# Scores copied out of PSUM by VectorE instead of ScalarE in an attention kernel with a computed position bias

## What is computed

```python
pos  = grid_q[:, :, None, :] - grid_kv[:, None, :, :]          # 1024 queries x 64 keys, x and y
bias = jnp.sign(pos) * jnp.log1p(jnp.abs(pos))
bias = relu(bias @ cpb_w1 + cpb_b1)                            # first layer, 2 -> 32
bias = relu(bias @ cpb_w2 + cpb_b2)                            # second layer, 32 -> 32
bias = (bias @ cpb_w3 + cpb_b3).reshape(b, 8, 1024, 64)        # third layer, 32 -> 1
sim  = einsum('bhid,bhjd->bhij', qh, kh) + bias
out  = einsum('bhij,bhjd->bhid', softmax(sim), vh)             # then projection, residual, MLP, residual
```

## Time and profile before

| | us |
|---|---|
| runs of the kernel before | 897.69, 897.99, 899.03 (median 897.99) |
| the profiled execution | 897.46, of which span from first to last instruction 895.7 |
| busy: PE, DVE, ACT, POOL | 814.1, 712.5, 675.4, 66.1 |
| mean granted TensorE clock | 0.975 of full speed |

### The profile page before, as it was taken

How to read it: one execution, slowest core, us unless ns; L and a number is a source line. 1 busy time by engine, 2 the same in 40 slices (tenths; PEclk the granted TensorE clock), 3 DMA queues, 4 the chain that set the end, 5 groups by cost and what they waited for, 6 DMA issues and landing times.

```text
span 895.7 us, 27530 instructions
## 1 busy us (share of the span) xinstructions
PE 814.1 (91%) x12470; PEld 232.7 (26%) x12470; DVE 712.5 (80%) x498; ACT 675.4 (75%) x775; POOL 66.1 (7%) x39
## 2 busy tenths in 40 slices
PE   2399998899999999789999999889999999999997
PEld 1122222232222222223222222222222222222224
DVE  4888798797877588888885868879888668989843
ACT  2468788878776688897876877797878678888863
POOL 3300031300000004030000000311000000000000
PEclk7599999999999999999999999999999999999999
DMA  4502020020110202002020200202002020200000
GB/s 163 120 2 49 2 48 4 12 65 3 43 34 1 48 3 49 12 3 65 2 63 15 49 1 3 49 12 53 15 4 61 14 48 2 72 3 2 2 15 25
DMA packets 18264, 27.67 MB, mean 31 GB/s; under 512 B 10980, under 2 KB 11620, under 8 KB 18148
## 3 DMA queue, kind: packets, MB, share of 16 engines
q1 hardware_dynamic: 18148, 25.91, 11.8%
HBM read 23.05 MB, written 2.74 MB: 29 GB/s over the span
## 4 chain that ended last, share of the span: by engine, by line
issue 59%; PE 26%; POOL 6%; ACT 5%; DVE 3%; DMA 0%; SPq 0%; ACTq 0%; POOLq 0%
PE pair L892 9%; PE scores L910 8%; POOL conv_prod L357 4%; ACT h L489 3%; POOL big L470 2%; PE pair L866 2%; DVE h L643 2%; PE pair L1045 1%; PE scores L921 1%; PE pair L1000 1%; PE pair L1018 1%; PE pair L1036 1%; PE scores L1006 1%; ACT big L591 0%; DMA const<-consts_dram 0%
## 5 line engine op out<-in xcount | busy, mean ns | idle before, releaser
L643 DVE TENSOR_TENSOR h<-hxy 128x2048 f32<-128x2048 f32 x256 | 578.4, 2288 | 76.5 <-PE pair L892 72.4
L489 ACT ACTIVATE h<-pair 128x1024 f32<-128x1024 f32 x512 | 517.2, 1023 | 143.5 <-PE pair L866 108.1
L892 PE MATMUL pair<-h,wts 32*32 32x512 f32 x8192 | 300.1, 603 | 17.0 <-ACT h L489 5.5
L910 PE MATMUL scores<-h,wts 128*32 128x512 f32 x2048 | 277.5, 610 | 0.1
L866 PE MATMUL pair<-fy,u_rows 32*128 32x512 bf16 x1024 | 103.1, 389 | 14.5 <-DMA fy<-fy_dram 14.5
L866 PEld LDWEIGHTS pair<-fy,u_rows 32*128 32x128 bf16 x1024 | 26.4, 91 | 233.6 <-issue 233.6
L892 PEld LDWEIGHTS pair<-h,wts 32*32 32x32 f32 x8192 | 66.1, 103 | 78.9 <-ACT h L489 34.5
L910 PEld LDWEIGHTS scores<-h,wts 128*32 128x32 f32 x2048 | 42.4, 108 | 157.5 <-issue 148.8
L357 POOL TENSOR_TENSOR conv_prod<-qpad,wts 128x288 f32<-128x288 f32 x16 | 34.0, 2150 | 426.5 <-ACT qpad L516 426.5
L1000 PE MATMUL pair<-const,probs 128*128 128x128 f32 x128 | 21.2, 291 | 21.5 <-ACT h L489 20.8
L499 ACT ACTIVATE probs<-scores,wts 128x512 f32<-128x512 f32 x32 | 22.0, 688 | 23.8 <-PE scores L910 23.5
(11 more groups left out here) (101 smaller groups left out, 376.0 us busy)
## 6 DMA issues: line engine op xcount, KB each, us to landing
hxy<-features_dram SPq DMA_DIRECT2D x64, 256.0 KB, 4.9
wts<-weights_dram SPq DMA_DIRECT2D x2, 960.0 KB, 8.1
att_den<-reciprocals_dram SPq DMA_DIRECT2D x7, 256.0 KB
x<-x_dram SPq DMA_DIRECT2D x2, 512.0 KB, 5.5
fy<-fy_dram SPq DMA_DIRECT2D x16, 64.0 KB
fy_dram<-fy_part SPq DMA_DIRECT2D x24, 32.0 KB, 3.8
out_dram<-x SPq DMA_DIRECT2D x3, 256.0 KB, 5.4
features_dram<-pos_sign SPq DMA_DIRECT2D x4, 128.0 KB, 2.3
```

The lines of the kernel that those rows point to most:

```text
L489: emptied("z", 2 * g + j, act.activation(h2[j][g % H2_BUFS][:].rearrange("p r n -> p (r n)"), pair_of("z", 2 * g + j)[:], ACT.Relu))
L643: dve.tensor_tensor(h1[g % H1_BUFS][:].rearrange("p c (y x) -> p c y x", x=W), hx[unit % 2][:, :, t].unsqueeze(2).broadcast_to([128, CT, H ...
L892: ins = pe.matmul(z_of(g, r)[32 * c:32 * (c + 1)], w(l, "w2")[key_rows(r), key_rows(r)], h1[g % H1_BUFS][key_rows(r), c], start=r >= 2, st ...
L910: ins = pe.matmul(scores[phase % 2][32 * r:32 * (r + 1)], w(l, "w3")[:, 32 * t:32 * (t + 1)], h2[rows[0] // 2][step % H2_BUFS][:, r % 2], ...
```

## The change

`copy_scores` moves from ACT to DVE and becomes a tensor-scalar add with the same operands. It gets a slot: 3, that is behind `first_layer(G+1)` and ahead of `first_layer(G+2)`, one slot ahead of `score_max`. Its three waits (the scores full, the products of queries and keys added, the earlier readers of `probs` done) move with it and now stand in DVE's list. Where a slot holds several stages, they follow in the order in which `plan` enters them: the stages behind a segment (`residual2`, `divide`) first, then those of the softmax, `hidden_terms`, and those of the next segment (`hats`).

```diff
-SOFTMAX_SLOTS = {("pe", "scores_t"): 2, ("dve", "score_max"): 4, ("act", "widen_max"): 3,
+SOFTMAX_SLOTS = {("dve", "copy_scores"): 3, ("pe", "scores_t"): 2, ("dve", "score_max"): 4, ("act", "widen_max"): 3,
                  ("pe", "max_off"): 4, ("act", "exp"): 4}
...
-            def copy_scores(phase):
-                unit, h = phase // 2, phase % 2
-                seg = unit // PAIRS
-                act.wait_ge(bias_added, STRIDES * (phase + 1) + 1)
-                act.wait_ge(qk_added, phase + 1)
-                if seg:
-                    wait_filled(act, "attend", 2 * (seg - 1) + h)
-                act.activation(probs[:, unit % PAIRS, bank(h)], scores[phase % 2][:], ACT.Identity, bias=w(seg // B, "b3"))\
-                    .then_inc(scores_copied, 1)
...
-                if g > STRIDES and g % STRIDES == 1 and g <= ALL_STEPS + 1:
-                    copy_scores(g // STRIDES - 1)
...
+            def copy_scores(phase):
+                unit, h = phase // 2, phase % 2
+                seg = unit // PAIRS
+                dve.wait_ge(bias_added, STRIDES * (phase + 1) + 1)
+                dve.wait_ge(qk_added, phase + 1)
+                if seg:
+                    wait_filled(dve, "attend", 2 * (seg - 1) + h)
+                dve.tensor_scalar(probs[:, unit % PAIRS, bank(h)], scores[phase % 2][:], w(seg // B, "b3"), None, ALU.add)\
+                    .then_inc(scores_copied, 1)
...
-                      "score_max": score_max, "divide": divide, "reciprocal": reciprocal,
+                      "copy_scores": copy_scores, "score_max": score_max, "divide": divide, "reciprocal": reciprocal,
```

## The result

The changed kernel takes 912.85 us (median of 4 runs, 911.56 to 914.74) against 898.51 for the kernel before on the same chip: a ratio of 1.0161, 95% interval 1.014 to 1.0182. That is slower, as forecast, but by 14 us and not by 5, and outside the range of 899.0 to 908.0. The profiled execution took 912.67, span 910.9, mean granted clock 0.972.

What follows compares the result with a forecast made beforehand. PE, busy 91% of the span, sets the time. Terms 0.36 - 3.42 - 2.01 - 0.42 + 0.15 - 0.06 gave 5.4 us lost: 903.4 beside the median of 897.99 (902.9 profiled); 8-in-10 range 899.0 to 908.0.

Steps and rivals of the forecast that it cites:

- the copy: Tensor-scalar out of PSUM on DVE: 0.75 us long, 0.67 from its start to the next DVE instruction (its turn).
- plain phases: 18 ordinary phases: layer3(G-1) to layer2(G+1) takes 3.66 us instead of 3.68, a gain of 0.02 each, 0.4 in all.
- divide in the chain: 6 phases (7 and 0) where divide stands ahead of score_max: loss 0.57 us each, 3.4 in all.
- the backlog: Phase 2 of segment 0, where DVE runs seven tiles without a pause: loss 0.42 us.
- the tail: The last phase, with nothing beside it: the copy takes 0.75 us for 0.69, loss 0.06.
- ACT's gain is taken by DVE's chain: Plain phases: ACT's relief lets PE run 0.29 us earlier, but copy, tile and maximum in sequence on DVE take it.
- layer2's wait for the maximum: Sign of being right: about 0.3 us in plain phases, 0.8 in six with divide, over 1 behind the convolution.
- Phase 4, 3 phases: Copy ahead of hats in slot 43; score_max at 389.70 against 389.75: gain 0.05 us each, 0.15 in all.
- Behind the convolution: Phase 3 of segments 0 to 2: DVE is late, so the copy's whole 0.67 us adds to layer2's wait; 2.0 in all.
- the clock: Rival, 20%: granted clock falls behind the convolution after longer PE idle time, costing 1 to 5.2 us; 904.4 to 908.6.
- the faster copy: Rival, 12%: out of PSUM the copy takes 0.42 to 0.55 us, say 0.48; 3.2 us gained, 894.8.
- PE did keep its clock in phase 4: Rival, 15%: earlier transposes keep PE's lead and clock in three phases 4, 2 us gained each; 897.4 to 903.

Runs made afterwards that it cites:

- E3: The changed kernel with score_max ahead of divide in the slots that hold both; 910.17 us, ratio 1.0128.
- E11: The changed kernel with phase 2 of segments 0 to 2 copied by ACT, phase 3 still by DVE; 910.37 us, ratio 1.0133.
- E6: The changed kernel with copy and score_max both last in slot 3, ahead of first_layer(G+2); 918.46 us, ratio 1.0221.
- E10: The kernel before, with copy and score_max early on DVE (slot 3) in 16 plain phases only; 894.96 us, ratio 0.9965.
- E1: The changed kernel with the copy behind hats, not ahead, in phase 4 of segments 0 to 2; 906.85 us, ratio 1.009.
- E9: The kernel before, ACT still copying, with only the copy's wait added in its slot on DVE, no work behind it; 902.88 us, ratio 1.0045.
- E2: The changed kernel with phase 3 of segments 0 to 2 copied by ACT; 909.21 us, ratio 1.0115.
- E8: The changed kernel with phase 3's copy in segments 0 to 2 one slot earlier, behind conv_sum and ahead of the tile; 913.04 us, ratio 1.0162.

## Why the prediction was wrong

Right, with sizes: the copy (0.75 taken, 0.750 measured; turn 0.67 and 0.67); plain phases (gain 0.02 forecast, 0.03 measured, as layer2's starts have it); divide in the chain (0.57; 0.58, and E3 shows that it is divide's place); the backlog (0.42; 0.40, gone in E11); the tail (0.06; 0.07). Also the reading that ACT's gain is taken by DVE's chain: E6 and E10 get the 0.29 us that were said to be there as soon as the tile leaves the chain. Of the signs that it named, layer2's wait for the maximum is 0.19 in plain phases for 0.3, 0.8 in those with divide as given, and behind the convolution, for "over 1 us", nothing, since layer3 at half clock covers it (0.82 in E3, where the clock holds). One sign of being wrong came true: PE waits for tiles of `first_layer`.

Wrong, the step "Phase 4, 3 phases ... Gain 0.05". It followed DVE's list to score_max, found that the copy fits into the idle time (it does, 4.54 for 4.50), and took the list behind score_max as unchanged. The idle time was not empty: POOL's products ran in it. With hats, which release them, 1.8 us later against layer3 and no idle time left ahead of score_max, POOL runs into the tile and the second hats, and these get 1.1 us longer each. That makes -1.5 a phase for +0.05, 4.85 us in all. Shown by E1 (hats back ahead: loss gone, same work) and E9 (hats held by a wait alone: 0.8 to 1.1 of loss, with POOL's 9.9 us in two of three segments). Two sentences of the forecast came near: that DVE's tiles leave 0.08 us at step 48, and that POOL shares DVE's list in time; they were used only to doubt a gain.

Too small, the term "Behind the convolution", 0.67 a phase. It is the right price of that phase's own copy (E11: 0.65, 0.66). It lacks the 0.3 to 0.5 by which phase 2's copy delays the convolution through POOL, DVE and POOL in each other's way at another place, some 1.2 us in all; and the clock, which was a rival with 20%: it fell in all three segments and cost 0.8, 0.7 and 1.5 more (1.70, 1.79 and 2.68, less the 0.91, 1.13 and 1.14 of E3, where it holds), 3.0 in all, within the 1 to 5.2 worked out for it. The reason given, PE's longer idle time ahead of the transposes (2.86 measured, 2.4 counted), is not the cause as far as the runs go: in E3 the clock holds in all three segments with that time at 2.84 to 2.86, in E2 and E10 it falls with 2.04 as before, and E8, which shortens it to 1.38, keeps the fall in two of three. What makes it fall stays open.

The sum: 4.85 + 1.2 + 3.0, and 0.88 ahead of step 9, are 9.9 us; the profiled execution took 912.67, 9.8 above the 902.9 forecast for it.

The other two rivals: the faster copy is out (750 ns). PE did keep its clock in phase 4 of segments 0 and 1, and its lead there (`layer2` of step 8p+12 comes 1.68 us earlier) is gone by step 8p+16, since the tiles of DVE set the end: the cover of 0.08 us said so.

## What to carry to other kernels

Idle time of an engine that is about to take more work is not free until one has looked at what the neighbour that slows it, and that it slows, does in just that time: here POOL's products lay in DVE's pause, and the forecast looked at DVE alone. A wait that moves ahead of a producer (hats) costs what that producer releases, work or no work. And an edit that is one line in a table of 32 phases is best judged by kind of phase: the same move gains 0.29 us in 18 of them and loses up to 3.9 in others (E6), and the version that keeps it only where it gains was the one that beat both kernels.

## What the runs showed of the hardware

- DVE and POOL slow each other. The tile (128x2048, two operands in SBUF) takes 2.28 us alone and 3.36 beside POOL's product, the hats (128x2048, one tensor) 1.22 and 2.30, hidden_terms 0.75 to 0.81 and up to 1.86; POOL's four products take 7.40, 7.95 or 9.92 us, and its four of the convolution 9.96, 10.44 or 12.15, with how much of DVE's work lies beside them. The Trainium skill (SBUF — State Buffer, Who interferes with whom) has DVE and GpSimd share a pair of ports that one of them holds for a whole instruction, for DVE instructions with two SBUF inputs or in a mode that uses two ports. The trace agrees in these rows; which instruction held the pair is not recorded.
- The granted clock falls or stays behind the same idle time of PE. In phase 3, with 2.04 to 2.05 us of it ahead of the transposes, the clock fell in none of three segments before, in one of three in E9, in two of three in E10 and in all three in E2; with 2.84 to 2.88 us, in none of three in E3, in two of three in E1 and in all three in the changed kernel. The fall costs 0.8 to 1.0 us there by itself (E9, E10), and 1.5 in segment 2 of the changed kernel, where it lasts twice as long. What decides it stays open; E8, the one run made to ask, only excludes that a shorter idle time ahead of the transposes is enough to keep it.
